# A recommender kernel: weight blocks turned on chip, products of zeros before the tiles, six fewer matmuls a tile, three row buffers

## What is computed

```python
emb = embed_table[f_ix, x_idx]                       # 2048 x 26 x 16
lin1 = w1_table[f_ix, x_idx].sum(axis=1) + w1_bias
fm = 0.5 * ((s * s).sum(-1) - (emb * emb).sum(axis=(1, 2)))        # s = emb.sum(axis=1)
h = relu(emb.reshape(n, 416) @ mlp_w1 + mlp_b1)      # 400 wide
h = relu(h @ mlp_w2 + mlp_b2)
mlp_out = h @ mlp_w3 + mlp_b3
last = x0 = emb.transpose(0, 2, 1)
for W in (cin_w0, cin_w1, cin_w2):                   # W is 128 x (26 or 128) x 26
    last = einsum('ndl,ndf,klf->ndk', last, x0, W); feats.append(last)
y = lin1 + fm + mlp_out + concat(feats).sum(axis=1) @ lin_w + lin_b
```

## Time and profile before

| what | us |
|---|---|
| median of 3 runs | 530.52 (530.10 to 530.93) |
| the profiled execution, its own time | 530.45 |
| its span, first to last instruction | 528.6 |
| PE busy | 468.6 |
| DVE busy | 376.7 |
| ACT busy | 361.6 |
| POOL busy | 364.6 |

### The profile page before, as it was taken

The page is one execution under the profiler, slowest core; times in us unless marked ns, Lnnn a source line. Parts: engine busy times, 40 slices in busy tenths (PEclk is TensorE's granted clock), DMA queues, the critical chain, the costliest instruction groups (busy, mean ns, idle before and its releaser), DMA issues. The chain is left out here.

```text
span 528.6 us, 6627 instructions
## 1 busy us (share of the span) xinstructions
PE 468.6 (89%) x2230; PEld 384.6 (73%) x2230; DVE 376.7 (71%) x610; ACT 361.6 (68%) x707; POOL 364.6 (69%) x382
## 2 busy tenths in 40 slices
PE   0798499899898989899999989898989899998895
PEld 0795367588787878687877878787868687787684
DVE  6811265869687786868686968778686868695766
ACT  1002459878686877777676868786777767677883
POOL 5777787877777777777777777777777777774000
PEclk9999559899999999999999999999999999999998
DMA  8973652122222222222222222222222222221000
GB/s 179 237 133 26 82 132 8 5 8 7 9 7 9 7 8 7 9 7 9 7 8 7 8 8 8 8 8 8 8 8 8 8 8 7 8 8 6 0 2 1
DMA packets 21550, 13.63 MB, mean 26 GB/s; under 512 B 12792, under 2 KB 20493, under 8 KB 21261
## 3 DMA queue, kind: packets, MB, share of 16 engines
q0 software_dynamic: 12064, 3.31, 18.4%
q1 hardware_dynamic: 5863, 7.92, 6.4%
q10 hardware_dynamic: 3590, 1.99, 2.0%
HBM read 13.00 MB, written 0.19 MB: 25 GB/s over the span
## 5 line engine op out<-in xcount | busy, mean ns | idle before, releaser
L417 POOL DMA_INDIRECT emb<-rows,idx_raw x377 | 364.3, 966 | 117.4 <-issue 114.6
L660 DVE TENSOR_TENSOR z_lo<-ps_s,z_hi 128x512 fp32r<-128x512 f32 (+1 forms) x192 | 130.7, 687 | 66.5 <-ACT ps_s L483 65.1
L476 ACT ACTIVATE z_hi<-ps_s 128x512 fp32r<-128x512 f32 (+1 forms) x192 | 114.4, 596 | 78.7 <-PE ps_s L908 77.8
L483 ACT ACTIVATE ps_s<-ps_s 128x512 f32<-128x512 f32 (+1 forms) x192 | 113.9, 593 | 0.7
L922 PE MATMUL ps_q<-z_lo,zw_hi 128*127 128x512 f32 (+1 forms) x192 | 86.0, 448 | 15.9 <-DVE z_lo L660 14.4
L923 PE MATMUL ps_q<-z_hi,zw_lo 128*127 128x512 f32 (+1 forms) x192 | 76.4, 398 | 0.0
L924 PE MATMUL ps_q<-z_hi,zw_hi 128*127 128x512 f32 (+1 forms) x192 | 76.3, 397 | 0.0
L908 PE MATMUL ps_s<-xt,pick 128*128 128x512 f32 (+1 forms) x192 | 74.3, 402 | 0.4 <-DVE xt L652 0.4
L922 PEld LDWEIGHTS ps_q<-z_lo,zw_hi 128*127 128x127 f32 (+1 forms) x192 | 36.4, 190 | 32.4 <-DVE z_lo L660 19.7
L994 PE MATMUL ps_y<-look_hi,one_hot 128*128 128x442 f32 (+1 forms) x156 | 56.3, 361 | 2.3 <-DVE one_hot L754 2.3
L995 PE MATMUL ps_y<-look_lo,one_hot 128*128 128x442 f32 (+1 forms) x156 | 54.8, 353 | 0.0
(11 more groups left out here) (165 smaller groups left out, 757.2 us busy)
## 6 DMA issues: line engine op xcount, KB each, us to landing
emb<-rows,idx_raw POOLq DMA_INDIRECT x377, 3.0
w_space<-rows SPq DMA_DIRECT2D x2, 728.9 KB
m_raw<-mlp_w SPq DMA_DIRECT2D x2, 650.0 KB
w<-cin_w SPq DMA_DIRECT2D x1, 832.0 KB, 6.7
w<-cin_w ACTq DMA_DIRECT2D x1, 832.0 KB, 13.2
w_space<-cin_w SPq DMA_DIRECT2D x1, 832.0 KB, 15.0
w_space<-cin_w ACTq DMA_DIRECT2D x1, 832.0 KB, 18.4
m_raw<-rows SPq DMA_DIRECT2D x1, 728.9 KB
```

The lines of the kernel that those rows point to most:

```text
L417: pool.indirect_dma_start(emb[t % EMB][:, f, :], None, rows, bass.IndirectOffsetOnAxis(row_ix[:, t, f:f + 1], 0)).then_inc(gathered[t], 16)
L476: act.activation(z_hi[0:k, c, :], ps[0:k, :], ACT.Square)
L483: act.activation(ps[0:k, :], ps[0:k, :], ACT.Square).then_inc(hi_ready, 1)
L660: dve.tensor_tensor(z_lo[0:k, u % NC, :], ps_s[s_no(t, u) % RING][0:k, :], z_hi[0:k, u % NC, :].bitcast(F32), ALU.subtract).then_inc(lo_re ...
```

## The change

1. **Weights turned on chip.** `cin_w2` and `cin_w1` come in halves; ACT and DVE (four `tensor_scalar` of 128x13x64 on DVE, L755 of the new kernel) write them turned, so that a weight slice is contiguous; the matmuls are 52 instead of 26 for each tensor, with 64 weight columns each.
2. **Moves in one piece.** Six stores (`leave`) and six loads (`move`) replace 3 stores and 62 loads.
3. **Products of zeros.** 28 matmuls of all-zero operands stand on PE ahead of its wait for `total` (WARM).
4. **Layer 1's low parts in pairs.** ACT copies `xt` to `x_two`, two blocks above one another (two copies of 52x512 a tile), and the low product takes 4 matmuls instead of 8. **Layer 2** takes 10 instead of 12: three blocks of 128 rows and one of 81 that holds the rest.
5. **Look-ups.** The keys are transposed once, stored to DRAM and read back spread over all partitions (`key_row`, in SBUF). The 39 `keys` matmuls of the tiles go; `one_hot` is made from `key_row` instead of from PSUM, in two buffers, at other units. The third `pick_row` moves ahead of `z_low(t, 0)`.
6. **Last tile.** Tile 15 is no longer started inside tile 14: after unit 11 come `hidden2(14)`, `sum_products(14)`, and then `x_half`. Its copy by position waits for 18 gathers, then for the last five.
7. **Row buffers** EMB 4 to 3; several buffers share room. `x_full` (the copy `x32`) moves behind `square(t, 0)`, the sum of `emb`'s last column to the tile's start.

```diff
+EARLY = 18
-        EMB = 4
+        EMB = 3
-        LOOK_SPLIT = {4: 0, 6: 1, 8: 2}
-        KEYS = {1: 0, 5: 1, 9: 2}
+        LOOK_SPLIT = {3: 0, 5: 1, 7: 2}
+        KEYS = {3: 0, 6: 1, 10: 2}
         ROWS = {3: 0, 7: 1, 11: 2}
-        PICKED = {5: 0, 9: 1}
+        PICKED = {6: 0, 10: 1}
+        WARM = 28
...
-                                            ).then_inc(gathered[t], 16)
+                                            ).then_inc(gathered[t] if t < T - 1 or f < EARLY else gathered_late, 16)
...
+            def x_pairs(t):
+                act.activation(x_two[0:XR], xt[t % 2][0:XR, 0:C8:2, :].bitcast(F32), ACT.Copy)
+                act.activation(x_two[LO:XK], xt[t % 2][0:XR, 1:C8:2, :].bitcast(F32), ACT.Copy).then_inc(x_two_ready, 1)
...
             def start_tile(t):
                 x_high(t, 0)
                 x_high(t, 1)
-                for u in range(NC):
-                    square(t, u)
+                square(t, 0)
+                x_full(t, 0)
+                x_full(t, 1)
+                square(t, 1)
+                square(t, 2)
+                x_pairs(t)
+                sum_first(t)
...
+            def turn(here, raw, in_sem, out_sem, h):
+                dve.wait_ge(in_sem[h], 16 * 2)
+                dve.tensor_scalar(turned(here, h, 1), turning(raw, h, 1), 1.0, None, ALU.mult).then_inc(out_sem[h], 1)
...
             def keys_to_one_hot(t, i):
-                dve.wait_ge(keys_out, look_no(t, i) + 1)
-                dve.tensor_tensor(one_hot[:], ps_y[:, 0:P].unsqueeze(1).to_broadcast([P, SHARES, P]),
+                if i == 0:
+                    dve.wait_ge(keys_in[t % 2], 16 * ((t - FIRST_LOOK) // 2 + 1))
+                n = look_no(t, i)
+                if n >= 2:
+                    dve.wait_ge(rows_out, n - 1)
+                dve.tensor_tensor(one_hot[n % 2][:], key_row[t % 2][:, i:i + 1, :].to_broadcast([P, SHARES, P]),
                                   share_row.unsqueeze(2).to_broadcast([P, SHARES, P]),
                                   ALU.is_equal).then_inc(one_hot_ready, 1)
...
-                for c in range(C8):
-                    mm = pe.matmul(ps_mlp[:, 0:H], x[0:96, c, :], m1_lo[0:96, c, :], start=False, stop=(c == C8 - 1))
+                pe.wait_ge(x_two_ready, t + 1)
+                for c in range(C8 // 2):
+                    mm = pe.matmul(ps_mlp[:, 0:H], x_two[0:XK, c, :], m1_lo[0:XK, c, :], start=False,
+                                   stop=(c == C8 // 2 - 1))
...
                 else:
+                    if after == T - 1:
+                        hidden2(t)
+                        sum_products(t)
+                        x_half(after, 0)
+                        x_half(after, 1)
                     picked(after, 0)
-                    hidden2(t)
+                    if after < T - 1:
+                        hidden2(t)
                     picked(after, 1)
                     picked(after, 2)
```

More of the change, by code:

```diff
@@ L206, in deepfm_cin_kernel @@
         look_place = sb("look_place", [P, T, LOOKS])
-        one_hot = sb("one_hot", [P, SHARES, P], F32R)
+        room_b = sb("room_b", [P, 8 * P])
+        key_row = [room_b[:, b * LOOKS * P:(b + 1) * LOOKS * P].rearrange("p (i n) -> p i n", i=LOOKS) for b in range(2)]
+        key_t = sb("key_t", [T * LOOKS, P])
+        one_hot = [sb(f"one_hot{b}", [P, SHARES, P], F32R) for b in range(2)]
         w2 = sb("w2", [P, K, F])
@@ L352, in move_lin, with turning, turned @@
                                   [[st_a, n_a], [2 * NX_, n_a], [1, n]])).then_inc(moved_in[g], 16)
+        def turning(mat, h, e):
+            return mat[:, HALF_P * h:HALF_P * (h + 1), HALF * e:HALF * (e + 1)].rearrange("p k f -> p f k")
+        def turned(mat, h, e):
+            return mat[:, HALF * e:HALF * (e + 1), HALF_P * h:HALF_P * (h + 1)]
         @block.sync
@@ L368, in _ @@
             sp.dma_start(m1_raw[LO:XK, :, :], by_pair).then_inc(m1_in, 16)
[L369 to L375, removed]
-            sp.wait_ge(moved_zeroed, 1)
[L377 to L381, removed]
+            sp.dma_start(m1_raw[ONE:ONE + 1, C8 - 2, :], mlp_b1.rearrange("(o h) -> o h", o=1)).then_inc(m1_in, 16)
+            for n, copies in enumerate((1, 1, 1, 2, 2, 3)):
+                sp.wait_ge(y_copied, copies)
+                leave(sp, n)
+            sp.wait_ge(moved_zeroed, 1)
+            move(sp, 0)
+            move(sp, 1)
+            sp.wait_ge(y_stored[6], 16)
             move_lin(sp, 0, F2, N2, 0, 0, N2)
             move_lin(sp, 0, F3, N3, 0, X12, N3)
-            move(sp, 1, XO + X12, N1, N3, N2, y12_dram, X12 + X13, W, N3, N2 * W)
+            move(sp, 2)
             W = 2 * NX_
@@ L576, in _ @@
             square(0, 2)
+            x_pairs(0)
+            sum_first(0)
             for t in range(T):
@@ L728, in tile, with start_last @@
                             pick_row(t + LEAD, PICKED[u])
-                        if u - 2 in KEYS:
-                            keys_to_one_hot(t + LEAD, KEYS[u - 2])
+                        if u in KEYS:
+                            keys_to_one_hot(t + LEAD, KEYS[u])
+            def start_last():
+                t = T - 1
+                times_left(t - 1, NQ - 1)
+                times_third(t - 1)
+                add_third(t - 1)
+                add_product(t - 1, NQ - 1)
+                fold(t - 1)
+                hidden2(t - 1)
+                x_low(t, 0)
+                x_low(t, 1)
+                for u in range(NC):
+                    z_low(t, u)
             def start_tile(t):
@@ L1011, in _ @@
                     pe.matmul(o, ident[0:k, 0:k], fm[0:k, j:j + 1], start=False, stop=False)
+            for n in range(WARM):
+                pe.matmul(ps_s[2][:, 0:2 * (XK + LO)], zw_hi[:, 0, :], zt_hi[:].rearrange("p e c -> p (e c)"),
+                          start=True, stop=True)
             for g in range(3):
@@ L1049, in _ @@
                     if looks(t + LEAD):
-                        if u in KEYS:
-                            keys(t + LEAD, KEYS[u])
                         if u in ROWS:
                             look_rows(t + LEAD, ROWS[u])
-                    if after is not None:
+                    if after is not None and after < T - 1:
                         if u == 9:
```

361 lines of the change are left out of this document (240 added, 121 removed).

## The result

The changed kernel takes 529.05 us (median of 12 runs, 527.89 to 529.94), where the kernel before took 530.52 beside it: a ratio of 0.997, 95% interval 0.9963 to 0.9978. That is 1.5 us less, within 0.05 us of the forecast. The profiled execution took 528.71 us for a span of 526.9. One of the 12 executions of experiment 4's kernel took 873.74 us; nothing here shows why, and its ratio leaves it out.

What follows compares the result with a forecast made beforehand. POOL's 377 gathers were taken to bound the kernel: 447.7 us to tile 14's last gather, plus S 13.6, is 461.3; plus 65.8 to the end, a span of 527.1; with 1.85 around it, forecast 529.0 us, range 522.0 to 536.5.

Steps and rivals of the forecast that it cites:

- The gathers pace the kernel: POOL's 377 gathers, one each 1.249 us, take 28.7 us a tile and set the time from about tile 2 on.
- Start and tiles priced at zero: Quicker first tile and quicker compute in every tile count 0 us, being hidden under POOL's gathers.
- The tile's 26.6 us: Compute for a tile with look-ups after the change: 26.6 us against POOL's 28.7.
- 25 us forward: First tile's unit 0, at 77.1 us before, comes perhaps 25 us earlier, at about 50 us.
- from tile 2 or 3: Sign in the new profile: ACT's by_pos copies wait for DMA, 1 to 4 us a tile, from there on.
- the 55: Worth of start and tiles were the gathers' cover gone: 25 + 15 x 2 = 55 us.
- S: Sum of what holds gathers up until tile 14 is in: 6.6 + 2.0 + 5.0 = 13.6 us.
- The tail: From tile 14 being in to the end of the span: 65.3 us, with 0.5 added for low clock 65.8.
- C: Rival at the gathers: one_hot holds nothing up; 524.0 us, or 522 without the turning's share; chance 0.20.
- B: Rival: one_hot meets the gathers' point of need at two of a tile's three places, 534 us, or three, 540; chance 0.22.
- D: Rival at the last two tiles: they overlap better, fold and sum done when the last gather lands; 524.7 us; chance 0.08.
- E: Rival: compute still paces, 528 to 530 us, or gathers are quicker than counted, 477; chance 0.05.

Runs made afterwards that it cites:

- experiment 4: The changed kernel with six more products of 400 columns a tile in layer 1: 528.91 us, ratio 0.9973.
- 5: The changed kernel with 39 of 377 gathers left out from tile 3 on, those columns holding old rows: 505.69 us, ratio 0.9539.
- 1: The changed kernel with share_row copied once into ps_y, so one_hot reads one input from PSUM and also waits for PE's products: 523.56 us, ratio 0.9872.
- 3: The changed kernel without turned weights, PE reading w2 and w1 with a stride: 526.22 us, ratio 0.9933.
- 10: Kernel 7 with its long two-input DVE instructions (look_lo, m1_lo, m2_lo) cut into pieces of some 0.5 us: 514.56 us, ratio 0.9703.
- 9: The changed kernel with turned weights multiplied over all 128 columns at once, 52 passes instead of 104: 528.35 us, ratio 0.9964.
- 2: The changed kernel with the last tile begun like the others, sum_products of tile 14 after unit 1 of tile 15: 523.3 us, ratio 0.9865.
- 6: The changed kernel without the 28 zero products (WARM 0): 528.37 us, ratio 0.9965.
- kernel 7: The changed kernel with three edits together: one_hot's share_row from PSUM, last tile begun like the others, no turning: 517.13 us, ratio 0.9749.

## Why the prediction was right, point by point

**The gathers pace the kernel: right.** It is shown from three sides: more compute changes nothing (4), fewer gathers give 505.69 (5), and each microsecond taken off the gathers' chain comes off the time (1, 3, 10).

**Start and tiles priced at zero: right in price, wrong in size.** The tile's 26.6 us was measured as 26.66. The step that failed is "25 us forward" for the start, a figure with no working behind it: it came 7 us forward. So the copies wait for gathers only from tile 5 on, not from tile 2 or 3. I had taken turned weights for quick ones, but these products take nearly the same time for the same number of columns loaded, 10.8 to 11.9 us (9), and the turn delays the first product by 3.3 us (3). Of the 7 us, 0.4 are there when `b_a` is copied (39.96, before 40.34); the rest comes behind it, with the moves: the last sum of moved pairs ends at 56.4 instead of 64.4. With gathers left out, so that the cover is gone, the change is worth 24.5 us, not 55: 505.69 (5) beside 530.20 for the kernel before. By layer 1 of tile 14 that kernel is 30.8 us ahead of before (451.15 against 481.95), but by that of tile 15 only 24.3 (482.15 against 506.42). The 6.5 us lost in between, where tile 15 is now begun late, are a term that the 55 left out. The error cost the forecast nothing because the start is hidden: it moved by -2.1 and +3.9 us (3, 9) with no sign of its own in the time.

**S: 13.6 forecast, 13.15 measured.** `one_hot` 5.0 against 4.64, the turning 2.0 against 1.7, `look_lo` 3.8 against 4.1, `m1_lo` 1.7 against 1.9, `m2_lo` 0.8 against 0.7. Tile 14 was copied at 460.66 instead of 461.3. That these came so near is partly luck. For the turning the forecast took the middle between holding nothing and an estimated 1.7 us a piece; each lasted 1.0 us and did hold gathers. For `one_hot` it had a chance of 0.46 and a mean wait of 0.28 us; 25 of 39 met a gather (0.64), for 0.19 us each. As expected, the places repeat in nearly every tile. In twelve of the thirteen tiles the first costs 0.1 to 0.2, the second nothing, the third about 0.2; other phases, bad ones too, were open. That a `one_hot` of 0.68 us holds the point for only 0.57 was not worked out from any row; the traces bear it out, since one that began up to 0.07 us after a gather's start held nothing (three rows of kernel 4).

**The tail: 65.8 forecast, 66.2 measured, by errors that nearly cancel.** Copy to unit 0 of tile 14 took 10.8, not 9.2. `picked` 1 and 2 wait there for the `x_full` copies, which I had counted at the last tile only; the changed kernel's timeline of PE:

```profile
469.12 1.08 PE L1091 MATMUL ps_s<-xt,pick 128*128 128x512 f32 x2 [0.43 <-ACT x L574]
```

Unit 0 to unit 11 took 17.1, not 19.3: ACT's squares did not set it, and PE's 18 us was nearer. The rest was 5.2, 6.3, 19.8 and 7.1 us against 4.9, 5.4, 19.4 and 7.1. I had added 0.5 for a low clock there, and PE did run units 0 and 1 of tile 15 at a granted clock of 0.50, at 0.63 us a matmul, 0.43 apart, where later ones last 0.39. The start of tile 15 (6.3) and its units (19.8) are together 1.3 us over; how much of that is the clock was not separated.

**The rivals.** C, that `one_hot` holds nothing up, is excluded by the 25 long gathers and by (1): with two SBUF inputs a gather 0.32 us behind `one_hot` took 1.17 us, with one it took 0.95. The Trainium skill's page "SBUF — State Buffer" (Who interferes with whom) infers that a `tensor_tensor` with two SBUF inputs does not stall a DMA of GpSimd, since making descriptors needs the write interface. With that inference this case disagrees. B did not come about, by phase. D did not: the last gather landed at 489.4 and the fold was not done until 493.6; its idea was worth 4.4 us of span once the order was changed (2). E's gathers were not quicker than counted.

## What to carry to other kernels

When one engine issues transfers back to back, gains on the other engines that lie under its chain are worth nothing until the chain gets shorter; find out with a kernel that leaves some of its work out, and one that adds work to the others. Look on that engine for rows longer than their median and see which instruction of another engine ends at a fixed distance before each: an input moved to PSUM gave 5.5 us, shorter pieces 2.6. And put what the last stage waits for first in every engine's order: sums and folds of the stage before can follow it (4.4 us of span).

## What the runs showed of the hardware

- A gather (indirect DMA issued by POOL, 0.944 us, 0.305 us of issue ahead of it) is held by a DVE instruction with two SBUF inputs that began before the gather's start and still runs 0.12 us after it, and ends 0.81 to 0.82 us after that instruction; such an instruction in the gather's second half does nothing (112.96 above). In the changed kernel all 25 `one_hot` that met a gather so held it; with one input in PSUM none of 26 did (1), nor any of 15 in the kernel before.
- `tensor_scalar` from SBUF to SBUF, one input, holds gathers as well: the gather of 11.57 ends 0.73 us after it. One that had started 0.11 us before such an instruction (14.70) ended with it, at 15.82. Kernels 1, 2, 4, 5, 6 and 9 show ten more like it, of gathers that began 0.02 to 0.49 us before it and ended within 0.03 us of its end, so a later part of a gather is held too. A two-input instruction in the same place held nothing: in kernel 7 a `look_lo` of 1.88 us began 0.13 us after a gather's start, and the gather took 0.94.
- The stride of 26 elements cost these weight loads nothing: 128 turned columns took 332 ns (9), and 128 with the stride 321, by the groups by form of kernel 3:

```profile
L1006 PEld LDWEIGHTS ps_y<-lin,w 128*128 128x128 f32 x52 | 11.8, 321 | 12.8 <-issue 12.8
```
